# Sparsemax threshold search: chunk-maxima statistics and a logarithmic secant in place of a sharpening pass and a count

## What is computed

```python
def sparsemax(x):
    x = x - jnp.max(x, axis=-1, keepdims=True)
    zs = -jnp.sort(-x, axis=-1)
    L = x.shape[-1]
    rho = jnp.arange(1, L + 1, dtype=x.dtype)
    cssv = jnp.cumsum(zs, axis=-1) - 1.0
    support = zs > cssv / rho
    k = jnp.maximum(jnp.sum(support, axis=-1, keepdims=True), 1)
    tau = jnp.take_along_axis(cssv, k - 1, axis=-1) / k.astype(x.dtype)
    return jnp.clip(x - tau, 0.0)
...
scores = jnp.einsum('bhqd,bhkd->bhqk', qh, kh) * scale
attn = sparsemax(scores)
out = jnp.einsum('bhqk,bhkd->bhqd', attn, vh)
```

## Time and profile before

| | us |
|---|---|
| median of 3 runs | 6964.34 |
| lowest and highest | 6961.25, 6969.25 |
| the profiled execution | 6963.19 |
| its span in the trace | 6961.2 |
| DVE busy | 5982.4 |
| ACT busy | 5612.5 |
| PE busy | 5170.4 |
| POOL busy | 2477.8 |

### The profile page before, as it was taken

One profiled execution on the slowest core, in us unless ns is written; L12 is line 12 of the kernel. 1 busy time (PEld: TensorE's weight loads), 2 busy tenths in 40 slices (PEclk: granted clock), 3 DMA queues, 4 the chain that ended last, 5 costly groups with the idle time before them and its releaser, 6 DMA issues. The chain is left out here.

```text
span 6961.2 us, 167719 instructions
## 1 busy us (share of the span) xinstructions
PE 5170.4 (74%) x20066; PEld 1708.2 (25%) x20067; DVE 5982.4 (86%) x50050; ACT 5612.5 (81%) x12612; POOL 2477.8 (36%) x10299
## 2 busy tenths in 40 slices
PE   8985776776777777776777777776777767779794
PEld 5551111111111111111111111111111111168573
DVE  5558999999999999999999999999999999935445
ACT  3327998998999999998999999999999999922231
POOL 2222333333333333333333333333333333323431
PEclk9996666676676666667666666766776776689897
DMA  5761111111111111111111111111111111054235
GB/s 197 239 203 49 31 31 29 33 32 28 32 33 31 31 31 31 31 30 28 31 31 30 32 32 31 31 31 30 32 32 33 32 32 34 22 191 174 90 100 189
DMA packets 370146, 416.60 MB, mean 60 GB/s; under 512 B 118688, under 2 KB 286240, under 8 KB 368672
## 3 DMA queue, kind: packets, MB, share of 16 engines
q1 hardware_dynamic: 355872, 370.61, 18.9%
q0 software_dynamic: 13056, 35.74, 1.4%
HBM read 249.13 MB, written 156.88 MB: 58 GB/s over the span
## 5 line engine op out<-in xcount | busy, mean ns | idle before, releaser
L872 DVE MAX8 a_cand<-a_scores 128x8 f32<-128x42 f32 (+1 forms) x38912 | 4389.0, 194 | 176.7 <-issue 132.9
L625 ACT ACTIVATE a_junk_act<-a_cand,a_ntau 128x304 f32<-128x304 f32 (+1 forms) x3840 | 1934.9, 523 | 143.3 <-POOL a_ntau L949 50.3
L595 PE MATMUL a_ring<-a_q,a_k 99*128 99x512 bf16 (+1 forms) x3328 | 1464.4, 553 | 765.6 <-ACT a_scores L660 490.0
L540 PE MATMUL a_out<-a_attn,a_v 128*16 128x512 f32 (+1 forms) x6656 | 1415.6, 792 | 505.3 <-ACT a_attn L664 505.3
L660 ACT COPY a_scores<-a_ring 128x1024 f32<-128x1024 f32 (+1 forms) x2048 | 1613.5, 832 | 151.9 <-PE a_ring L591 85.6
L664 ACT ACTIVATE a_attn<-a_ring 128x1024 f32<-128x1024 f32 (+1 forms) x1792 | 1656.3, 977 | 2.8 <-PE a_ring L595 2.4
L591 PE MATMUL a_ring<-a_k,a_q 96*128 96x512 bf16 (+1 forms) x4096 | 1345.6, 456 | 87.9 <-DVE a_ident L685 33.0
L625 ACT ACTIVATION_READ_ACCUMULATOR a_junk_act<-a_cand,a_ntau 128x1 f32 x3840 | 803.6, 209 | 0.0
L591 PEld LDWEIGHTS a_ring<-a_k,a_q 96*128 96x128 bf16 x4096 | 384.5, 117 | 1471.4 <-ACT a_attn L664 692.0
L595 PEld LDWEIGHTS a_ring<-a_q,a_k 99*128 99x128 bf16 (+1 forms) x3328 | 287.5, 118 | 1597.0 <-ACT a_scores L660 863.9
L540 PEld LDWEIGHTS a_out<-a_attn,a_v 128*16 128x16 f32 (+1 forms) x6656 | 136.4, 100 | 1184.4 <-ACT a_attn L664 713.1
(11 more groups left out here) (227 smaller groups left out, 6414.5 us busy)
## 6 DMA issues: line engine op xcount, KB each, us to landing
a_k<-k_parts SPq DMA_DIRECT2D x1536, 50.0 KB
k_parts<-p_ks SPq DMA_DIRECT2D x48, 800.5 KB, 7.2
o_parts<-a_o SPq DMA_DIRECT2D x1024, 32.0 KB, 1.6
e_o<-o_parts SPq DMA_DIRECT2D x64, 512.0 KB, 6.5
p_ctx<-in_ctx_t SPq DMA_DIRECT2D x16, 1601.0 KB, 8.3
v_heads<-p_v SPq DMA_DIRECT2D x16, 1536.0 KB
a_q<-q_parts SPq DMA_DIRECT2D x1536, 16.0 KB
a_v<-v_heads SPq DMA_DIRECT2D x256, 96.0 KB
```

What stands on the lines that cost most here:

```text
L540: mm = nc.tensor.matmul(out_ps[at:at + HEAD_DIM], v_st[0:rows, u, c], attn[0:rows, k, (c % 2) * BANK:(c % 2 + 1) * BANK], start=c < 4, sto ...
L595: mm = nc.tensor.matmul(at[0:rows, m * BANK:(m + 1) * BANK], k_st[0:SCORE_ROWS + TAU_ROWS, ut, c * P:c * P + rows], q_st[0:SCORE_ROWS + TA ...
L625: ins = nc.scalar.activation(into[:, t].rearrange("p (a b) -> p a b", b=CHUNKS), cand[:, u % SLOTS, t, 0:w], ACT.Relu, bias=ntau[:, u % 2, ...
L872: ins = V.max(cand[:, u % SLOTS, t, :, c], scores[:, u % SLOTS, t, lo:hi])
```

## The change

`start` on DVE now takes BN_STATS of the 38 chunk maxima, four times, adds the two parts of the squared spread and reduces the eighth values (`tops`, now alone). The rest is POOL's: `guess` (the threshold of round 0 linear in mean and variance, and with a POW a first estimate of the slope `per_fall`), `first`, and then twice `factors` and `improve`, a secant in the logarithm of the excess. Each `factors` needs a reciprocal of a `square` that DVE computes (`inverse`, in tile 2 and in tile 3). Round 0 on ACT measures the top six of each chunk (228 columns) instead of the top four; in the last round ACT measures two tiles and DVE two. BEFORE_LAST goes from 3e-4 to 4.5e-4. The fallback reduces the first candidates itself (`g_lead`).

```diff
-FIRST, SECOND = 2, 4
-USUAL_COUNT = 22.0
+SECOND = 6
+GUESS_AT, GUESS_SPREAD = 0.0202, 6.42
+FALL_AT, FALL_SPREAD = 0.0035, 0.693
+NEAR = 0.03, 0.001
-BEFORE_LAST = 3e-4
+BEFORE_LAST = 4.5e-4
-ACT_LAST = 3
+ACT_LAST = 2
...
             def start(i, u, link):
-                c, nt = cand[:, u % SLOTS], ntau[:, u % 2]
...
-                V.tensor_reduce(tops[:, u % 2].rearrange("p r t -> p t r"), c[:, :, 0:8:7], AX.X, ALU.max, negate=True)
-                yield from link(V.tensor_reduce(w1[:], c[:, :, 0], AX.X, ALU.add))
-                yield from link(V.tensor_scalar(nt, w1[:], -1.0 / CHUNKS, None, ALU.mult))
-                for t in range(TILES):
-                    ins = measure_own(t, c[:, t, 0:FIRST], CHUNKS * FIRST, nt)
+                c, st = cand[:, u % SLOTS], stats[:, u % 2]
+                for t in range(TILES):
+                    ins = V.bn_stats(st[:, t], c[:, t, 0])
                 yield from link(ins)
...
+                V.tensor_tensor(spread_sq[:, u % 2], st[:, :, 2], st[:, :, 5], ALU.add).then_inc(spread_made, 1)
+                V.tensor_reduce(tops[:, u % 2], c[:, :, 7], AX.X, ALU.max, negate=True)
+
+            def inverse(i, n):
+
+                dve.wait_ge(square_made, 2 * i + n + 1)
+                V.reciprocal(square_inv[:], square[:]).then_inc(inv_made, 1)
...
+                link(V.tensor_reduce(g_lead[:], firsts, AX.X, ALU.max, negate=True))
...
+                    if t == 2 and has(i, 1):
+                        inverse(i - 1, 0)
+                        yield
                     if t == 2 and has(i, 2):
                         yield from settle(i - 2, last, link)
                     if t == 3 and has(i, 1):
-                        for _ in range(5):
+                        for _ in range(2):
                             yield
-                        yield from slope(i - 1, prev, link)
+                        inverse(i - 1, 1)
...
+                def factors(i, u, n, fall, rise):
+
+                    G.tensor_scalar(half[:], fall, -0.5, None, ALU.mult)
+                    pool.wait_ge(inv_made, 2 * i + n + 1)
                     pool.sem_inc(passed_pool, 1)
...
+                    link(G.tensor_tensor(share[:], rise, square_inv[:], ALU.mult))
+                    link(G.tensor_tensor(linear[:], share[:], fall, ALU.mult))
+                    link(G.tensor_tensor(cubic[:], linear[:], share[:], ALU.mult))
+                    G.tensor_tensor(linear_b[:], linear[:], half[:], ALU.add)
+                    G.tensor_tensor(cubic_b[:], cubic[:], linear[:], ALU.subtract)
...
+                def improve(i, u, r, fall, next_fall, over):
+
+                    nt = ntau[:, u % 2]
+                    pool.wait_ge(excess_made, ROUNDS * i + r + 1)
                     pool.sem_inc(passed_pool, 1)
...
+                    link(G.tensor_scalar(over[:], excess[:, u % 2, r], 1.5, -1.0, ALU.min, ALU.add))
+                    link(G.tensor_tensor(term[:], over[:], cubic_b[:], ALU.mult))
+                    link(G.tensor_tensor(term[:], term[:], linear_b[:], ALU.add))
+                    link(G.tensor_tensor(term[:], term[:], over[:], ALU.mult))
+                    link(G.tensor_tensor(next_fall, term[:], fall, ALU.add))
+                    link(G.tensor_tensor(move[:], over[:], next_fall, ALU.mult))
                     G.tensor_tensor(nt, nt, move[:], ALU.subtract).then_inc(tau_tried, 1)
...
+                prev, fall = (u - 1) % U, per_fall[:, (u - 1) % 2]
+                if has(i, 1):
+                    guess(i - 1, prev)
                 if has(i, 2):
                     last_step(i - 2, (u - 2) % U)
                 if has(i, 1):
-                    second(i - 1, (u - 1) % U)
-                    third(i - 1, (u - 1) % U)
+                    first(i - 1, prev)
+                    factors(i - 1, prev, 0, fall, rise[:])
+                    improve(i - 1, prev, 1, fall, fall1[:], over1)
+                    link(G.tensor_tensor(square[:], over1[:], over1[:], ALU.mult))
+                    G.tensor_scalar(square[:], square[:], NEAR[1] ** 2, None, ALU.add).then_inc(square_made, 1)
                 if has(i, 2):
                     divide_up(i - 2, (u - 2) % U)
                 if has(i, 1):
-                    slope(i - 1, (u - 1) % U)
+                    factors(i - 1, prev, 1, fall1[:], over1[:])
+                    improve(i - 1, prev, 2, fall1[:], fall, over)
```

## The result

| | before | after |
|---|---|---|
| median of 4 runs each, same chip, us | 6966.80 | 7311.29 |
| lowest and highest | 6961.25, 6971.32 | 7306.24, 7317.52 |
| ratio, 95% interval | | 1.0495 [1.0477, 1.0513] |
| span of the profiled execution | 6961.2 | 7304.4 |
| L651 (now L653), first to last start | 5513.3 | 5852.9 |

What follows compares the result with a forecast made beforehand. ACT was taken to set the step, with DVE 0.46 us behind, and ACT and POOL after the change. +172 (step) - 50 (edges) + 165 (fallback) = +287 us, giving 7251 us, range 7100 to 7390.

Steps and rivals of the forecast that it cites:

- What bounds, and the new wait: ACT sets the step; POOL's longer chain between rounds 1 and 2 makes it wait 0.95 us: step 21.12, +172 us.
- ScalarE's sums: ACT's measures: last round -0.53 us, first round +0.25, in all -0.28, giving ACT 20.17 us per step.
- The timetable: Times within a step: first square 12.3 us, second 18.5, last threshold 2.8 into the next; DVE 18.35 us per step.
- The loop edges: DVE's stall at the 21 loop edges fits its slack: 2.5 of 3.57 us gone at each, -50 us.
- The counts: Fallback: 71 tiles flagged in 64 heads, 96 full measures and 25 Newton steps, against 45 and 4 before.
- The fallback: DVE's flagged-tile load of 585 us, less 2.9 absorbed per head, gives 399; less the 234 of now, +165 us.
- The held link: The 51 added full measures could each hold a POOL link 1.65 us, 84 us if uncovered; taken as covered.
- A: Rival: POOL's chain is hidden and only sums count, 20.17 us per step; 7078 us; 12%.
- C: Rival: DVE's two waits bind, POOL's further lateness returns through DVE, 0.5 us per step more; 7380 us; 15%.
- B: Rival: DVE's lag after a flag is absorbed over three score slots; faster from 3.6 us per head; 5%.
- D: Rival: the counts of flags don't hold because bn_stats or POW round otherwise; 6995 us at old counts; 3%.

Runs made afterwards that it cites:

- the short and the long chain: Changed kernel with `improve` rewritten to four waits instead of six, 7188.6 us; changed kernel with one more link in round 1's `improve`, 7367.6 us.
- Without flags: Both bounds that make a row bad put out of reach, so the fallback never runs: changed kernel 6834.34 us, kernel before 6728.95 us.
- The early count alone: Changed kernel with PE's count of flagged rows put ahead of the value matmuls instead of behind them: 7273.41 us.
- the moved measure: Changed kernel with round 1 measured on ACT before the last large ReLU piece instead of after it: 7223.68 us.
- the ballast: Changed kernel with four unused 128x304 measures added on DVE in each step's tile 1: 7375.15 us.

## Why the prediction was right, and where it was not

**What bounds, and the new wait: right.** The step of 21.12 and the idle time before round 2 with L939 as releaser are as forecast, and the short and the long chain show the cause by dose (0.53 off the chain, 0.55 off the step; 0.38 and 0.36 on). 255 x 0.67 = 171 us (forecast 172). The exact agreement is luck, as said above: ACT's own work and its wait are each off by 0.12.

**ScalarE's sums: right.** ACT is busy 20.24 in the step (20.17 forecast). Round 0's measures start 0.47 apart at 228 columns; the half-way guess between 0.41 and 0.53 was good.

**The timetable: right within 0.2.** The first square ends at 12.37 (12.3), the second at 18.68 (18.5), the last round's threshold at 3.01 (2.8). Of the two prices for BN_STATS the lower, taken from the nearer shape, was right: four over 38 columns take 0.39 us from the first start to the next instruction's, about 0.10 each. DVE is busy 17.82 in the step.

**The loop edges: right.** -50 was the term. Without flags what is lost about the edges falls from 62 to 11 us, -51. The excess of the whole stage over undisturbed steps falls by 68 (71 to 3), so 17 us more went in steps away from the edges (6 of them in the first eight steps), for which the forecast had no term.

**The counts: right.** 96 full measures and 25 Newton steps.

```profile
L739 DVE SCALAR_TENSOR_TENSOR a_junk<-a_scores,a_ntau,a_zeros 128x1601 f32<-128x1601 f32 x96 | 181.3, 1889 | 76.8 <-issue 60.5 <-DVE a_flag_i L748 6.6 <-remote 6.0
...
L761 DVE SCALAR_TENSOR_TENSOR a_junk<-a_scores,a_ntau,a_zeros 128x1601 f32<-128x1601 f32 x25 | 47.2, 1889 | 19.0 <-DVE a_flag_i L748 19.0
```

**The fallback: the mis-sized term.** Forecast: 585 us of load less 2.9 absorbed per head, 399, so +165. Measured: 464 us by the traces and 477 by the medians, +234 to +239. 585 - 464 = 121 over 64 heads is 1.9 us absorbed, next to the low end (1.8) and not the 2.9 taken. That one step accounts for the miss: +69 to +74 here, less 18 for the edges and what went with them, is 51 to 56 of the 60 us. For a lone flagged tile the chain of the argument was right and its times were early. Head 89, one flagged tile and no Newton step, with its step begun at 2643.05; DVE, POOL and ACT:

```profile
2658.76 1.89 DVE L739 SCALAR_TENSOR_TENSOR a_junk<-a_scores,a_ntau,a_zeros 128x1601 f32<-128x1601 f32 x1 [0.89 <-issue]
...
2667.10 0.17 DVE L718 RECIPROCAL a_square_inv<-a_square 128x4 f32<-128x4 f32 x1
```

```profile
2658.81 1.89 POOL L934 TENSOR_TENSOR a_term<-a_over,a_cubic_b 128x4 f32<-128x4 f32 x1 [0.18 <-POOL a_over L933]
...
2671.22 0.20 POOL L939 TENSOR_TENSOR a_ntau<-a_ntau,a_move 128x4 f32<-128x4 f32 x1 [0.18 <-POOL a_move L938]
```

```profile
2662.65 0.55 ACT L627 ACTIVATE a_junk_act<-a_cand,a_ntau 128x304 f32<-128x304 f32 x1 [2.55 <-POOL a_ntau L939]
...
2671.45 0.55 ACT L627 ACTIVATE a_junk_act<-a_cand,a_ntau 128x304 f32<-128x304 f32 x1 [1.94 <-POOL a_ntau L939]
```

The forecast had the second reciprocal at 22.9 of the step; it starts at 24.05. The last round's threshold is there at 28.37 (26.9 forecast) and wanted at 24.6, so about 3.75 us are lost; the two steps take 22.81 + 23.18 = 45.99, 3.75 over 42.24. The lateness begins with PE's count: the full measure starts 15.7 into the step, in head 196, where the count was not late, at 14.6, and that head costs 2.61 us, close to what the forecast had (5.4 - 2.9 = 2.5). Head 196 is the cheapest of its kind. Step by step against the run without flags, the seven lone heads with one flagged tile (no other flagged head within two steps) cost 2.6 to 4.0 us, 3.3 in the mean, and the eight with a Newton step as well 10.8 to 11.9, 11.35 in the mean, where the forecast's figures give 2.5 and 10.5: with or without a Newton step a lone head absorbs 2.1 us. The early count alone gives 38 of the 65 to 78 us between forecast and measurement, takes head 89 to 22.30 + 22.74, 0.95 less, and brings a lone head to 2.4 absorbed. The other 0.5 us per head, some 30 us in all, stays open.

The way was other than forecast where a Newton step comes in. The forecast had all of the delay go through the last round's threshold. In 24 of the 25 heads with one ACT first stands 6.6 us or more before L662, for the score slot, in the same step, and only the rest is lost at thresholds. Over the stage the flags add 201 us of waits for the slot and 202 us of waits for L939.

**The held link: there; that it is covered, as taken, is not shown.** In head 89 ACT's first wait is 2.55 instead of 0.83, because POOL's L934 lasted 1.89 us instead of 0.20. The two waits of ACT in the rows above, 1.72 more than usual and 1.94, make up the 3.75 but for 0.1. With the first gone, the last round would be asked for earlier and wait longer. That this is so was worked out from the times of the head; no run removed the held link alone.

**The rivals.** A (POOL hidden) falls with steps of 21.12; the moved measure shows what it would take to come near it. (The range was said to reach to A, but A's 7078 lies below its end of 7100.) C (DVE's two waits bind) falls with the ballast: 2 us more of DVE's busy time, nearly no wait left before the reciprocals, same step. B's 3.6 us absorbed per head were 1.9; the score slots that were to absorb the lag hold ACT up instead. D's other counts did not come.

## What to carry to other kernels

A chain of small dependent operations on one engine costs its count of waits times the start-to-start time (here 0.38 us), however little the engine is busy; where the bounding engine has no slack ahead of its result, every link is paid in every step, and a formula with more operations and two waits fewer is faster. Before moving a search to cheaper statistics, count how often its correction path runs: here a threshold of tolerance was worth 257 us and the whole new wait 217. Slack absorbs a rare long detour only from the moment the detour starts, so ask what queue the flag that starts it stands in.

## What the runs showed of the hardware that was not expected

- **An operation of POOL stands for as long as a DVE instruction with two SBUF inputs.** L934 beside a full measure lasts 1.89 us, which is that measure's own span (both rows above), against a median of 0.20:

```profile
L934 POOL TENSOR_TENSOR a_term<-a_over,a_cubic_b x512: 200/200/1892, 574.8 to 6440.7; 128x4 f32<-128x4 f32 x171
```

  The Trainium skill (SBUF — State Buffer, Who interferes with whom) states this lock; the trace agrees. It falls on different links of the chain, L933 in head 196 and L934 in head 89, depending on when the flag is read.
- **The granted clock of PE moves work that is not a matmul.** Eight fp32 matmuls take 1.05 us at 1.00 and 1.91 at 0.50. In the two steps shown DVE learns of a flag 1.1 us later at the low clock, and these matmuls are most of that.
- **A POW on four elements per partition takes 1.04 us on POOL** (L901, 1036 to 1052 ns over 256), where a multiplication of the same shape takes 0.20. The operation that depends on it starts 1.23 us after it (5575.67 to 5576.90), for 0.38 after a multiplication. It was hidden here: later in the same step POOL stands 1.43 us for ACT (before L909).
- **Moving work on ACT can starve PE of PSUM slots.** Measuring round 1 before a ReLU instead of behind it made PE stand for 2.1 us in 25 of 55 undisturbed steps, and those steps take 20.7 to 21.2 us where the others, but for one, take 20.1 to 20.5.
